# Linear attention in a GPS graph layer: each head's kv folded into the output weight

## The reference, cut to what matters

```python
qkv = x @ W_qkv
q, k, v = jnp.split(qkv, 3, axis=-1)
q = rmsnorm(q, qn_w); k = rmsnorm(k, kn_w)
q, k, v = map(split_heads, (q, k, v))
q = jax.nn.relu(q); k = jax.nn.relu(k)
kv = jnp.einsum('bhnd,bhne->bhde', k, v)
out = jnp.einsum('bhnd,bhde->bhne', q, kv)
k_sum = k.sum(axis=2)
normalizer = jnp.einsum('bhnd,bhd->bhn', q, k_sum) + EPS_DEN
out = out / normalizer[..., None]
out = out.transpose(0, 2, 1, 3).reshape(b, n, DIM)
return out @ W_out + b_out
...
x = x + _L0_gnn_ref(xn, ...) + _L0_mix_ref(xn[None], ...)[0]
x = x + _L0_ffn_ref(_layernorm(x, axis=-1)[None], ...)[0]
```

## Time and profile before

| | us |
|---|---|
| median of 3 runs | 1120.47 (1119.83 to 1121.78) |
| the profiled execution | 1117.66 |
| its span, first to last instruction | 1115.9 |
| TensorE busy | 948.5 (85%) |
| VectorE busy | 758.8 (68%) |
| ScalarE busy | 302.0 (27%) |
| GpSimd busy | 195.0 (17%) |

### The profile page before, as it was taken

The page is one execution under the profiler, slowest core; times in us unless marked ns, Lnnn a source line. Parts: engine busy times, 40 slices in busy tenths (PEclk is TensorE's granted clock), DMA queues, the critical chain, the costliest instruction groups (busy, mean ns, idle before and its releaser), DMA issues.

```text
span 1115.9 us, 18538 instructions
## 1 busy us (share of the span) xinstructions
PE 948.5 (85%) x5609; PEld 590.9 (53%) x5610; DVE 758.8 (68%) x1231; ACT 302.0 (27%) x502; POOL 195.0 (17%) x220
## 2 busy tenths in 40 slices
PE   2526999999999989999788999999726989999993
PEld 1323666666666655555555666666524545555551
DVE  4889788888888889722777777776564545555551
ACT  0561222222222222533111121211101323333331
POOL 1133000000000010000323232223102233243321
PEclk9757899999999999999889999999957999999997
DMA  7544544333343331493135443535536996977553
GB/s 242 158 141 144 215 151 150 139 124 124 139 150 141 141 132 39 114 316 101 55 95 168 123 146 124 162 99 174 170 135 235 310 302 148 314 204 211 118 105 57
DMA packets 77814, 176.17 MB, mean 158 GB/s; under 512 B 24180, under 2 KB 39482, under 8 KB 73922
## 3 DMA queue, kind: packets, MB, share of 16 engines
q1 hardware_dynamic: 70001, 147.40, 39.3%
q0 software_dynamic: 7776, 28.32, 11.3%
HBM read 113.54 MB, written 62.67 MB: 158 GB/s over the span
## 4 chain that ended last, share of the span: by engine, by line
PE 21%; DVE 13%; DMA 8%; issue 6%; ACT 2%; POOL 1%; SPq 1%; DVEq 0%; POOLq 0%; ACTq 0%
PE windows L946 8%; PE bank L838 5%; DMA arena<-t_dram,arena 4%; DVE arena L1437 4%; DMA out_x<-arena 3%; PE bank L964 3%; PE bank L937 2%; PE bank L831 1%; PE windows L899 1%; DVE arena L1476 1%; DVE arena L1436 1%; DVE arena L1438 1%; DVE arena L1471 1%; ACT arena L1128 1%; PE windows L838 1%
## 5 line engine op out<-in xcount | busy, mean ns | idle before, releaser
L758 PE MATMUL bank<-arena 128*125 128x512 f16 x960 | 218.6, 385 | 0.0
L838 PE MATMUL bank<-arena 128*125 128x512 f16 x864 | 195.5, 384 | 1.8 <-POOL arena L616 1.8
L758 PEld LDWEIGHTS bank<-arena 128*125 (+1 forms) x960 | 130.0, 139 | 74.0 <-issue 5.1
L838 PEld LDWEIGHTS bank<-arena 128*125 (+1 forms) x864 | 118.5, 138 | 67.4 <-issue 3.0
L946 PE MATMUL windows<-arena 128*128 x648 | 149.4, 381 | 0.0
L814 PE MATMUL bank<-arena 128*128 128x416 f16 (+1 forms) x576 | 103.1, 338 | 0.0
L946 PEld LDWEIGHTS windows<-arena 128*128 128x128 f16 x648 | 63.6, 98 | 65.7 <-issue 1.3
L814 PEld LDWEIGHTS bank<-arena 128*128 128x128 f16 x576 | 55.5, 97 | 44.0
L964 PE MATMUL bank<-arena 128*128 x324 | 74.4, 379 | 2.3 <-DVE arena L1639 2.3
L1332 DVE TENSOR_TENSOR arena<-windows,arena 128x1024 f32 x49 | 59.8, 1220 | 22.1 <-issue 7.7
L616 POOL TENSOR_TENSOR arena<-arena 128x250 f32 (+1 forms) x40 | 27.1, 677 | 265.7 <-ACT arena L1109 265.7
(11 more groups left out here) (227 smaller groups left out, 1421.4 us busy)
## 6 DMA issues: line engine op xcount, KB each, us to landing
arena<-split_dram SPq DMA_DIRECT2D x56, 512.0 KB, 5.1
arena<-in_w_flat SPq DMA_DIRECT2D x22, 1024.0 KB, 6.4
split_dram<-arena SPq DMA_DIRECT2D x44, 512.0 KB, 3.7
arena<-in_w_flat SPq DMA_DIRECT2D x40, 256.0 KB, 3.6
split_dram<-arena SPq DMA_DIRECT2D x80, 128.0 KB, 2.3
arena<-in_x SPq DMA_DIRECT2D x20, 448.0 KB
arena<-in_w_qkv SPq DMA_DIRECT2D x8, 1024.0 KB, 6.4
t_dram<-arena SPq DMA_DIRECT2D x10, 448.0 KB
```

The source lines that it names most:

```text
L758: mm = pe.matmul(bank[b][0:TT, :], xt[:, l, k, tok(i)], wkv[:, r, k, c0:c0 + 512], start=(k == 0 and n == 0), stop=(k == KT - 1 and n == 2))
L838: mm = pe.matmul(o[half][0:TT, :], a_[:, l, k, tok(i)], w_[:, r, k, c0:c0 + 512], start=(m == 0 and k == 0 and c == 0), stop=(m == 1 and k ...
```

## The change

- After the last `kv_sums`, DVE takes the key sums (`key_sums`), their reciprocal, and q's norm weight times the key sums. It writes `kvn`, each head's kv with every row divided by its key sum, in fp32. PE transposes it (`kv_turn`, 8 transposes) after the third q group, and ACT and DVE split it into `kvt` after the fourth (`kvt_copy`, `kvt_lo`).
- In the last turn of the q stage, PE multiplies `kvt` into the output weight: `wo_fold(n)` for n = 0 to 15 (8 blocks by 2 halves of 512 columns), three matmuls each. ACT and DVE write the result over `wo` as new halves (`fold_hi`, `fold_lo`).
- q is kept as fp32 only, relu(q * weight * key sum), written once by ACT; DVE makes no low half of it.
- An attention unit is on PE one fp32 matmul of 250 columns with a matrix of zeros and ones (`head_mask`) that sums a head's 64 rows: the normalizer. DVE's third step multiplies q itself (in SBUF) by the reciprocal. ACT and POOL split the quotient as before, in place (`ut16`).
- The attention parts multiply the divided q with the folded `wo`.
- The low half of `wo` is loaded before the last q weight, and `wg` after it; the sum buffers of the squares have moved to free its place. The q loop of turns 2 and 3 is unrolled.

```diff
+            def kv_turn():
+                pe.wait_ge(kvn_ready, 1)
+                for p in range(PAIRS):
+                    mm = pe.transpose(bank[3 + p // 4][:, (p % 4) * P:(p % 4 + 1) * P], kvn[:, p, :], ident)
+                mm.then_inc(kvt_psum, 1)
+            def wo_fold(n):
+                k, half = divmod(n, 2)
+                if n == 0:
+                    pe.wait_ge(kvt_ready, 1)
+                    for hl in range(2):
+                        pe.wait_ge(wo_in[hl], 16 * N_PIECE_O)
+                if n >= 3:
+                    pe.wait_ge(m_done, n - 2)
+                for c, (l, r) in enumerate(((0, 0), (0, 1), (1, 0))):
+                    mm = pe.matmul(bank[3 + n % 3][:, :], kvt[:, l, k * P:(k + 1) * P], wo[:, r, k, half * 512:half * 512 + 512], start=(c == 0), stop=(c == 2))
+                mm.then_inc(m_mm, 1)
...
             def attend_unit(j, g, unit):
-                for at, w in ((0, kvb), (256, ksb)):
-                    for c, (l, r) in enumerate(((0, 0), (1, 0), (0, 1))):
-                        mm = pe.matmul(o[:, at:at + AW], w[l][:, j, :], ut[:, r, j, bass.ds(g * AW, AW)], start=(c == 0), stop=(c == 2))
+                pe.matmul(bank[2 + j % 2][:, 0:AW], head_mask, ut[:, j, bass.ds(g * AW, AW)], start=True, stop=True).then_inc(at_mm, 1)
...
             pe.wait_ge(eps_ready, 3)
+            pe.wait_ge(m_done, 2 * KT)
             pe.wait_ge(wg_in[1], 32)
...
-            for hl in range(2):
-                pe.wait_ge(wo_in[hl], 16 * N_PIECE_O)
             pe.wait_ge(at_done, START + PAIRS)
...
# SP
             sp.wait_ge(acc_out, 16 * 2 * KT)
-            load_wg()
+            load_wo(1)
             load_wq(3, 1)
+            load_wg()
...
             sp.wait_ge(eps_mm, 3)
-            load_wo(1)
...
# ACT, per q group
-                    a_.activation(ut[:, 0, bass.ds(2 * t + h, 1), a:a + n]..., bank[u % 3][:, 0:n], ACT.Relu,
-                                  scale=qnw[:, bass.ds(2 * t + h, 1)])
-                    a_.activation(u32[u % 2][:, 0:n], bank[u % 3][:, 0:n], ACT.Relu, scale=qnw[:, bass.ds(2 * t + h, 1)]).then_inc(q_evac, 1)
+                    a_.activation(ut[:, 2 * t + h, a:a + n], bank[u % 3][:, 0:n], ACT.Relu, scale=ks_sum[:, 2 * t + h:2 * t + h + 1]).then_inc(q_evac, 1)
+                    if first and u == 3:
+                        kvt_copy()
+                    if last:
+                        for m in folds(u):
+                            fold_hi(m)
...
# DVE
+            def fold_lo(n):
+                k, half = divmod(n, 2)
+                c = slice(half * 512, half * 512 + 512)
+                v.wait_ge(m_hi, n + 1)
+                v.scalar_tensor_tensor(wo[:, 1, k, c], bank[3 + n % 3][:, :], FOLD, wo[:, 0, k, c], ALU.mult, ALU.subtract).then_inc(m_done, 1)
...
             def q_unit(t, u):
-                v.wait_ge(q_evac, START + 6 * t + u + 1)
-                v.tensor_tensor(ut[:, 1, bass.ds(2 * t + h, 1), a:a + n]..., u32[u % 2][:, 0:n],
-                                ut[:, 0, bass.ds(2 * t + h, 1), a:a + n]..., ALU.subtract).then_inc(q_split, 1)
...
             def attend_unit(j, g, unit):
-                st.done(v.tensor_tensor(a, o[:, 256:256 + AW], eps_row[:, bass.ds(g * AW, AW)], ALU.add))
+                st.done(v.tensor_tensor(a, o[:, 0:AW], eps_row[:, bass.ds(g * AW, AW)], ALU.add))
                 st.done(v.reciprocal(a, a))
-                v.scalar_tensor_tensor(a, o[:, 0:AW], SX, a, ALU.mult, ALU.mult).then_inc(at_f, 1)
+                v.scalar_tensor_tensor(a, ut[:, j, bass.ds(g * AW, AW)], SQ, a, ALU.mult, ALU.mult).then_inc(at_f, 1)
```

More of the change, by code:

```diff
@@ L80 @@
 ST = 16.0
+SKV = 256.0
+SQ = 128.0
+FOLD = SX / (SQ * SKV)
 EPS_LN, EPS_Q, EPS_T = 1e-5, 1e-6, 1e-5
@@ L350, in row_of, with folds @@
             return rows3[bass.ds(i, 1)].rearrange("o p d -> (o p) d")
+        def folds(u):
+            return range(8 * u // 3, 8 * (u + 1) // 3)
         block = ctx.enter_context(nc.Block())
@@ L802, in _, with q_units @@
             kv_sums()
-            def q_units(t, groups=0):
+            def kv_turn():
[14 more added lines that the diff above has]
+                mm.then_inc(m_mm, 1)
+            def q_units(t, groups=0, first=False, last=False):
                 for u in range(6):
@@ L818, in q_units, with graph_part @@
                         steps(KV_GROUPS + 6 * t + u, u % 2)
[L819 removed]
+                    if first and u == 2:
+                        kv_turn()
+                    if last:
+                        for n in folds(u):
+                            wo_fold(n)
+            q_units(0, 6, first=True)
             q_units(1, Q_GROUPS - 6)
[L821 to L822 removed]
+            q_units(2)
+            q_units(3, last=True)
             def attend_unit(j, g, unit):
[L825 removed]
                 pe.wait_ge(at_f, START + (max(unit - 1, 0) if isinstance(unit, int) else unit - 1))
[L827 to L834 removed]
+                pe.matmul(bank[2 + j % 2][:, 0:AW], head_mask, ut[:, j, bass.ds(g * AW, AW)], start=True, stop=True).then_inc(at_mm, 1)
+            def graph_part(i, o, half, a, b):
                 c0 = half * 512
@@ L1095, in q_turn @@
                             acc_part_hi(k)
-            q_turn(0)
+            q_turn(0, first=True)
             q_turn(1, split=True)
-            with a_.Fori(2, KT // 2) as t:
-                q_turn(t)
+            q_turn(2)
+            q_turn(3, last=True)
             a_.wait_ge(acc_out, 16 * 2 * KT)
@@ L1392, in ks_hi @@
-            def ks_hi():
-                for p in range(PAIRS):
-                    ins = v.tensor_scalar(ksb[0][:, p, :], head_mask, ksf[:, p:p + 1], None, ALU.mult)
-                st.done(ins)
-            def ks_lo():
-                for p in range(PAIRS):
-                    ins = v.scalar_tensor_tensor(ksb[1][:, p, :], head_mask, ksf[:, p:p + 1], ksb[0][:, p, :], ALU.mult, ALU.subtract)
-                ins.then_inc(kvb_ready, 1)
+                    ins = v.tensor_scalar(ks_sum[:, 3 * b:3 * b + n], bank[3 + b][:, 0:390].rearrange("p (a b) -> p a b", b=130)[:, 0:n, P], 2.0 ** -12, 1e-30,
+                                          ALU.mult, ALU.max)
@@ new lines, in key_sums @@
+                st.done(ins)
+                st.done(v.reciprocal(ks_inv, ks_sum))
+                v.tensor_tensor(ks_sum, ks_sum, qnw, ALU.mult).then_inc(qk_ready, 1)
+                st.done(v.tensor_scalar(ks_inv, ks_inv, SKV * 2.0 ** -12, None, ALU.mult))
+                v.wait_ge(kv_zero, 4)
+                for b in range(3):
+                    n = min(3, PAIRS - 3 * b)
+                    for r0 in (0, 64):
+                        ins = v.tensor_tensor(kvn[r0:r0 + 64, 3 * b:3 * b + n, r0:r0 + 64],
+                                              bank[3 + b][r0:r0 + 64, 0:390].rearrange("p (a b) -> p a b", b=130)[:, 0:n, r0:r0 + 64],
+                                              ks_inv[r0:r0 + 64, 3 * b:3 * b + n].unsqueeze(2).to_broadcast([64, n, 64]), ALU.mult)
@@ new lines, in key_sums, with kvt_lo @@
+                ins.then_inc(kvn_ready, 1)
+            def kvt_lo():
+                for b in range(2):
+                    c = slice(4 * b * P, 4 * (b + 1) * P)
+                    v.wait_ge(kvt_hi, b + 1)
+                    ins = v.tensor_tensor(kvt[:, 1, c], bank[3 + b][:, :], kvt[:, 0, c], ALU.subtract)
+                ins.then_inc(kvt_ready, 1)
+            def fold_lo(n):
+                k, half = divmod(n, 2)
+                c = slice(half * 512, half * 512 + 512)
+                v.wait_ge(m_hi, n + 1)
+                v.scalar_tensor_tensor(wo[:, 1, k, c], bank[3 + n % 3][:, :], FOLD, wo[:, 0, k, c], ALU.mult, ALU.subtract).then_inc(m_done, 1)
@@ L1419, in q_turn @@
                     q_unit(t, u)
-                    if first and u in (1, 3, 4):
-                        (kv_split, ks_hi, ks_lo)[u // 2]()
+                    if first and u == 3:
+                        kvt_lo()
                     if split and u >= 3:
@@ L1424, in q_turn @@
                             acc_part_lo(k)
-            v.wait_ge(kvb_zero, 5)
+                    if last:
+                        for n in folds(u):
+                            fold_lo(n)
+            key_sums()
             q_turn(0, 6, first=True)
             q_turn(1, Q_GROUPS - 6, split=True)
-            with v.Fori(2, KT // 2) as t:
-                q_turn(t)
+            q_turn(2)
+            q_turn(3, last=True)
             def attend_unit(j, g, unit):
```

127 lines of the change are left out of this document (60 added, 67 removed).

## The result

The changed kernel took 1131.61 us (median of 5 runs) beside 1120.47 for the kernel before; the ratio of the runs is 1.0118, 95% interval [1.0098, 1.0138]. By the ratio that is 13 us slower (1120.47 x 0.0118, so 1133.7); the two medians lie 11.1 us apart. The forecast was 7.7 us slower, the range 1122.5 to 1133.5. So the direction was right; the time stands at the upper end of the range, the median just inside it and the ratio just outside, and the forecast's own sum was well short of both.

A forecast was written before the change was run, and what follows sets the result against it. PE alone bounds the q stage; mixing is PE's for eight units, then mostly DVE's. 10.4 + 0.9 - 1.5 - 0.4 - 1.5 - 1.3 + 0.3 + 0.8 = +7.7 us, median 1128.2, range 1122.5 to 1133.5.

The forecast's parts named there:

- Folds, +10.4: Last q turn: 48 fp16 matmuls of 512 columns on PE, 0.216 us each, nothing to hide in: +10.4 us.
- rival (b): Q stage: folds stall on the late low half of `wo` or on evictions; +6 us, 1134; chance 0.08.
- Q stage in all: Q stage on PE: folds +10.4, kv transposes +0.9, DVE no longer late -1.5, earlier sums-of-squares wait gone -0.4 us.
- First units, -1.5: Mixing stage's first stretch: seven units on PE count, each 0.42 us instead of 0.63 to 0.64: -1.5 us.
- Rival (a): Mixing stage: PE paces it all, so all 40 units count; -1.1 us, 1119.4; chance 0.14, 0.04 of it faster.
- Third step beside POOL, +0.3: Mixing loop: DVE's step, now reading SBUF, waits for POOL's additions; pauses take in most: +0.3 us over three rounds.
- Loop heads, -1.3: Mixing loop: only the two units heading PE's 14 us per round count, -0.44 us three times: -1.3 us.
- Clock, +0.8: Starts of attention parts: PE idles about 0.9 us longer; one more 1.2 GHz start an even bet, half of 1.7 us.
- The sign at the end of the working: Mixing loop: rounds longer than 54.5 us would show the forecast wrong, through POOL waits or cold starts in each.
- (c): Mixing stage: DVE's wait for POOL is not taken in, 1.7 us at four places; +6.8 us, 1135; chance 0.10.
- Its own low end: Forecast's range: 9.4 less 4.5 us, a unit at 0.21 where it counts, nothing lost to POOL or clock: 1125.4.

The follow-up runs named there:

- before_short: Kernel before with the three numerator matmuls of each unit left out, DVE's third step taking the normalizer; 1134.05 us, head to gates 209.14 us.
- bank_source: Changed kernel with DVE's third step reading the unit's PSUM bank instead of q in SBUF, leaving q out of the product; 1157.63 us.
- both: Changed kernel with 14 filler matmuls ahead of each head of the attention parts and DVE's mixing loop written out; 1124.95 us, ratio 1.0033.
- warm: Changed kernel with 14 unused matmuls of 512 columns ahead of the wait at each head of the attention parts; 1125.47 us, ratio 1.0048.
- unroll: Changed kernel with DVE's loop over the mixing stage's tiles written out, so the third step's source address is fixed; 1131.75 us, ratio 1.0098.

## Why the prediction was off

By its own steps:

- **Folds, +10.4**: right; 0.65 us each, 6.90 for 32 matmuls. No DMA and no bank made them wait, so rival (b) was out. The low half of `wo` was issued at 483.86, as foreseen, 14 us ahead of the first fold.
- **Q stage in all**: forecast 10.4 + 0.9 - 1.5 - 0.4 = 9.4, measured 128.83 - 119.93 = 8.90 between stages that began warm. The profiled run had 1.65 more from the cold start at 402; the same 1.93 to 1.94 us of idle time stood there in all 14 traces, and 5 of the 10 of the changed kernel and its variants were cold, and 1 of 4 of the kernel before (`before_short`). So it can fall on either kernel; whether the change makes it likelier is open.
- **First units, -1.5**: measured -1.79 from the sums of squares to the ninth unit. A turn is 3.01 us and the unit's two passes are 0.21 us apart, as foreseen.
- **Rival (a)**, TensorE setting all rounds: out; the rounds became longer, and from the ninth unit to the first head nothing came back.
- **Third step beside POOL, +0.3**: right. It does wait, as the prediction took from the row of the quarter (2.17 us), and the pauses take it in (0.2 us by `bank_source`). The rule of the Trainium skill (SBUF — State Buffer, "Who interferes with whom") agrees on both sides of this experiment: 1.50 to 1.80 us under POOL's additions with both sources in SBUF, 0.42 in all 40 steps with one in a bank.
- **Loop heads, -1.3**: right in kind. `before_short` shows 2.0 for units that are shorter still; with clock and register operation out of the way (`both`) rounds are the 53.3 us forecast. In the changed kernel itself nothing of it is left: the rest is 205.8 for 204.8, +1.0 where these two terms had made it -1.0.
- **Not in the sum**: the address of `ut` that depends on the loop's counter. 0.11 us in each of 24 units, six of them in the chain of a round by the 0.66 us between rounds of 54.0 (`warm`) and 53.35 (`both`); 1.1 to 1.9 us in all.
- **Clock, +0.8: the step that failed.** The prediction wrote "with PE idle about 0.9 us longer at each, one more is an even bet". TensorE idled 1.1 to 1.8 us longer at each, and all four heads were cold in both profiles: 9.6 us where the kernel before had 1.7, that is +7.9. The count was the larger miss: three more starts at the forecast's 1.7 us are 5.1. The price was the other: 1.7 is what a stretch of 3.4 us at 1.2 GHz costs, and two of the four heads had 6.8 us and cost 3.1 each. `warm` gives the term as time: 1.0118 or 1.0132 becomes 1.0048, which is 7.8 to 9.4 us.

Without its clock term the prediction was +6.9 us. The changed kernel with its heads kept warm is at +5.4 (1120.5 x 0.0048, interval 3.7 to 7.2) beside a kernel before that keeps its own cold head; with one such start of 1.7 in both it would be +7.1. The sign at the end of the working, "cold starts in each", was named as what rounds longer than 54.5 us would mean; they were 57.0, 55.7 and 56.5 (before: 53.7, 53.7 and, with the cold head, 55.0).

The range reached as far as it did for other reasons than the one that came true: its upper end took in parts of rivals (b) and (c), which were both out, and two more cold starts. That the median lies just inside it is luck. Its own low end was also worked out wrongly: a unit at 0.21 us gains 0.43 in 13 places, 5.6 us and not 4.5, which changes nothing here.

Why the bet was misjudged can be read in the earlier trace rows: at 2.08 us of idle time one head was warm and at 2.11 the next was cold. Where either can happen, half a cold start more was too little for waits that all grow by 1 us or more: of the 27 heads in these traces with more than 2.5 us of idle time, 25 were cold. The warm head after 3.37 us in the kernel before spoke the other way, and it was one of the two exceptions.

What stays open: why two of the four versions with VectorE's loop written out (`unroll`, `both`) reach the key sums 2 us earlier; what decides whether a start behind 1.9 to 3.4 us of idle time is cold; and +0.7 us between the ninth unit and the first head, of which the written-out loop and the bank as source take back 0.2 to 0.4.

## What to carry to other kernels

Shortening TensorE's work where TensorE is already the one that waits is not free: it lengthens the idle time, and the matmuls behind it can run at half the clock. Read the idle time ahead of each burst in the trace before; where some are already cold, take every one as cold after the change (here that would have given the count), and price it by cold rows, the dear ones too. Moving work from a place with slack (the units) to a stage where its engine is never idle (the folds) pays full price there and gives back little. And an operand indexed by a machine loop's counter adds to its instruction; look whether that instruction is in a chain.

## What the runs showed of the hardware that was not expected

- TensorE's clock behind an idle stretch, at these heads and at the key sums: warm after up to 1.92 us in every head here, either way after 1.93 to 2.11 (key sums 1.54 or 1.9 to 2.7 us for the same 24 matmuls; heads 5.34 or 6.4 to 6.5), cold after 2.6 to 6.0 in 25 of 27, but warm after 2.97 us in `before_short` and after 3.37 in the kernel before.
- The clock can fall when the engine is already at work again: between 1.1 us before and 1.3 us behind the first matmul at the cold heads. So a burst can begin warm and be slow behind (a unit of 0.68 us ahead of parts of 7.03 in `unroll`).
- The price of one cold head was 0.9 to 2.6 us for the same 24 matmuls. At every cold head the clock was low for 3.4 or 6.8 us, and the price is half of what falls on the matmuls.
- An fp32 matmul of 250 columns with 128 rows is two passes in 0.42 us, against 0.63 for six fp16 matmuls.
- The register operation of an address that depends on the loop's counter is shown on VectorE as 57 ns and moves the instruction's start by 0.11 us.
